# Context work in the first projection, weights split in the last turn of self-attention, later loads spread

## The reference

```python
x = x + attn(_layernorm(x)) @ w_out.T                         # self-attention, 2048 keys
x = x + cross(_layernorm(x), ctx_1024, ctx_1024, mask, ...)   # 154 context rows per batch
x = x + ffn(_layernorm(x), ...)                               # shared and selected experts
```

## Time and profile before

| | |
|---|---|
| median of 3 runs (range) | 3333.91 us (3328.81 to 3335.09) |
| the profiled execution | 3329.57 us, span 3327.8 us |
| busy in the span | PE 90%, DVE 66%, POOL 52%, ACT 49% |
| stage A | 0 to 314 us |
| stage B | 314 to 2138.5 us |
| stage C | 2138.5 to 2389.6 us |
| stage D | 2389.6 to 2430.4 us |
| stage E | 2430.4 to 2777.4 us |
| feed-forward stages | 2777.4 to 3327.8 us |

### The profile page before, as it was taken

One profiled execution on the slowest core, in us unless ns is written; L12 is line 12 of the kernel. 1 busy time (PEld: TensorE's weight loads), 2 busy tenths in 40 slices (PEclk: granted clock), 3 DMA queues, 4 the chain that ended last, 5 costly groups with the idle time before them and its releaser, 6 DMA issues. The chain is left out here.

```text
span 3327.8 us, 41873 instructions
## 1 busy us (share of the span) xinstructions
PE 2984.6 (90%) x15214; PEld 1715.5 (52%) x15214; DVE 2191.5 (66%) x3923; ACT 1620.7 (49%) x2965; POOL 1718.3 (52%) x693
## 2 busy tenths in 40 slices
PE   7997999999999999999999999499558995989478
PEld 6885444444444444444444444178434553777433
DVE  4333888788888888888888886156227894666323
ACT  2221366666666666666666666322116672222111
POOL 0001287888787888878787878500021001333265
PEclk9998699999999999999999999799769997999689
DMA  4445544655547446464464443468664343333621
GB/s 178 177 164 174 131 86 105 139 107 125 121 89 155 86 105 141 105 142 104 99 143 105 86 96 72 129 190 242 167 157 132 117 120 115 127 132 115 214 80 35
DMA packets 171869, 424.75 MB, mean 128 GB/s; under 512 B 19361, under 2 KB 40770, under 8 KB 151684
## 3 DMA queue, kind: packets, MB, share of 16 engines
q1 hardware_dynamic: 147550, 277.49, 28.6%
q0 software_dynamic: 24128, 144.75, 20.7%
HBM read 170.20 MB, written 124.58 MB: 89 GB/s over the span
## 5 line engine op out<-in xcount | busy, mean ns | idle before, releaser
L654 DVE TENSOR_REDUCE part_max<-ps_s 128x1 f32<-128x512 f32 x2048 | 1270.6, 680 | 308.7 <-PE ps_s L555 308.7
L751 ACT ACTIVATE probs<-ps_st 128x512 f32<-128x512 f32 x2048 | 1086.2, 601 | 547.0 <-PE ps_st L574 527.0
L513 POOL TENSOR_TENSOR added<-added,probs 128x2048 f32<-128x2048 f32 x256 | 1182.5, 4619 | 91.3 <-ACT probs L751 64.9
L555 PE MATMUL ps_s<-k_stack,q_stack 96*128 96x512 f32 x2048 | 841.5, 427 | 28.0 <-POOL max_parts L503 20.6
L574 PE MATMUL ps_st<-q_stack,k_stack 98*128 98x512 f32 x2048 | 858.2, 425 | 6.3 <-ACT probs L751 5.0
L574 PEld LDWEIGHTS ps_st<-q_stack,k_stack 98*128 98x128 f32 x2048 | 386.6, 190 | 505.3 <-ACT probs L751 362.8
L585 PE MATMUL ps_pv<-probs,v_sb 128*32 128x512 f32 x4096 | 546.3, 605 | 0.0
L555 PEld LDWEIGHTS ps_s<-k_stack,q_stack 96*128 96x128 f32 x2048 | 395.2, 193 | 214.8 <-DVE part_max L654 144.2
L521 POOL DMA_DIRECT2D probs<-probs x128 | 112.9, 882 | 231.6 <-PE ps_pv L585 219.3
L513 POOL TENSOR_TENSOR added<-probs 128x2048 f32<-128x2048 f32 x32 | 146.0, 4563 | 48.7 <-ACT probs L751 48.7
L679 DVE RECIPROCAL ps_d<-ps_d 128x128 f32<-128x128 f32 x128 | 120.9, 949 | 64.3 <-PE ps_d L600 64.3
(11 more groups left out here) (268 smaller groups left out, 3573.1 us busy)
## 6 DMA issues: line engine op xcount, KB each, us to landing
probs<-probs POOLq DMA_DIRECT2D x128, 1024.0 KB, 6.9
xq_stack<-q_parts SPq DMA_DIRECT2D x64, 384.0 KB, 4.5
q_stack<-q_hi SPq DMA_DIRECT2D x64, 256.0 KB, 6.0
k_stack<-k_hi SPq DMA_DIRECT2D x64, 256.0 KB, 8.1
q_parts<-q_h_out SPq DMA_DIRECT2D x64, 256.0 KB, 4.9
x_in<-in_x_rows SPq DMA_DIRECT2D x8, 1024.0 KB
q_hi<-qk_h_out SPq DMA_DIRECT2D x8, 1024.0 KB, 4.3
q_lo<-qk_l_out SPq DMA_DIRECT2D x8, 1024.0 KB, 6.4
```

The lines of the kernel that those rows point to most:

```text
L513: pool.tensor_tensor(added[:, w % 2], left, probs[:, k % RING], ALU.add).then_inc(added_up, 1)
L555: pe.matmul(ps_s[:, place % BANKS], q_stack[0:ROWS, w % 4, j, t * P:(t + 1) * P], k_stack[0:ROWS, w // BPB, j, n * BLK:(n + 1) * BLK], sta ...
L654: dve.tensor_reduce(part_max[:, s:s + 1], ps_s[:, (w * SLOTS + s) % BANKS], AX.X, ALU.max)\
L751: act.activation(probs[:, k % RING, j], ps_st[:, n % BANKS], ACT.Exp, scale=SCALE).then_inc(item_used, 1)
```

## The change

Stage D is gone. Its work goes into stage A: SP issues its ten loads behind the first block of x and the identity and ahead of the weights, and its stores behind the load of block 1; PE makes the keys before `transposes(0, 0)` and the values behind them; ACT adds the bias before `transposed(0, 0)`; POOL makes the high and low parts of the keys; DVE makes the masks between `norm(0, 0)` and `transposed(0, 0)`, and adds the values' bias between its weight splits. PSUM has two banks for it where stage D had eight. Stage B copies both weights of stage C to DRAM scratch at its start, loads them in the last turn at w = 3 into the free half of `k_stack`, with block 0 of the attention's output into that of `v_sb`; ACT makes their high parts in unit w = 6 at k = 4 and 11, DVE their low parts in w = 7. Stage C starts with the split of block 0. In stage E `load_q(2)` goes ahead of `rows_into_place(0)`, `load_q(3)` to u = 0, the batch-1 keys to u = 2 and 4, and the three weights to u = 6, 8 and 10.

```diff
# Ahead
-    def load(self, sp):
-        for source, raw, _, _ in self.weights:
-            sp.dma_start(raw, source).then_inc(self.loaded, 16)
+    def load(self, sp, n):
+        source, raw, _, _ = self.weights[n]
+        sp.dma_start(raw, source).then_inc(self.loaded, 16)
...
# project_qkv, SP
                 sp.dma_start(ident[:], eye).then_inc(ident_loaded, 16)
+                sp.dma_start(ctx_sb[:], weight_rows(ctx_t)).then_inc(ctx_loaded["k"], 16)
+                sp.dma_start(wk_sb, weight_rows(wk_t)).then_inc(ctx_loaded["k"], 16)
+                sp.dma_start(bk_sb[:], bk_cols).then_inc(ctx_loaded["k"], 16)
+                sp.dma_start(xwv_sb, weight_rows(xv_t)).then_inc(ctx_loaded["v"], 16)
+                sp.dma_start(bv_sb[:], bv.partition_broadcast(KH)).then_inc(ctx_loaded["v"], 16)
+                sp.dma_start(pad_col[:], pad_cols).then_inc(ctx_loaded["mask"], 16)
+                for b in range(B):
+                    sp.dma_start(pad_row[:, b], pad[b].partition_broadcast(P)).then_inc(ctx_loaded["mask"], 16)
+                sp.dma_start(cq, causal_q).then_inc(ctx_loaded["mask"], 16)
+                sp.dma_start(ck, causal_k).then_inc(ctx_loaded["mask"], 16)
...
                 sp.dma_start(x_in[:, 1], x_blocks[1]).then_inc(x_loaded[1], 16)
+
+                sp.wait_ge(k_low, B)
...
+                sp.wait_ge(v_ready, 2 * B)
+                sp.dma_start(xv_rows, xv[:]).then_inc(ctx_stored, 16)
+                sp.wait_ge(masks_done, 3 * B + 1)
...
# project_qkv, POOL
                 rsqrt(0)
+                pool.wait_ge(k_biased, DC)
+                for b in range(B):
+                    pool.tensor_copy(kt_h[:, b], kt[:, b]).then_inc(k_high, 1)
+                for b in range(B):
+                    pool.wait_ge(k_high, b + 1)
+                    pool.tensor_tensor(kt_l[:, b], kt[:, b], kt_h[:, b].bitcast(F32), ALU.subtract).then_inc(k_low, 1)
                 rsqrt(1)
...
# project_qkv, DVE (masks() is stage D's code)
+                def context_values(n):
+                    dve.wait_ge(ctx_v_done, n + 1)
+                    dve.wait_ge(ctx_loaded["v"], 32)
+                    dve.tensor_tensor(xv[:, n // 2, n % 2], ps_x[0:KH, n % 2], bv_sb[:], ALU.add).then_inc(v_ready, 1)
+
                 norm(0, 0)
+                masks()
                 transposed(0, 0)
+                for n in range(2):
+                    context_values(n)
                 for n, (raw, high, low) in enumerate(WEIGHTS):
                     dve.wait_ge(w_high, n + 1)
                     dve.tensor_tensor(low, raw, high.bitcast(F32), ALU.subtract).then_inc(w_low, 1)
+                    if n < 2:
+                        context_values(n + 2)
...
# project_qkv, PE
+                def context_keys(c):
+                    if c >= 2:
+                        pe.wait_ge(k_biased, c - 1)
...
+                def context_values(n):
+                    if n < 2:
+                        pe.wait_ge(k_biased, DC - 1 + n)
+                    else:
+                        pe.wait_ge(v_ready, n - 1)
...
+                pe.wait_ge(ctx_loaded["k"], 48)
+                for c in range(DC):
+                    context_keys(c)
                 pe.wait_ge(ident_loaded, 16)
                 transposes(0, 0)
+                pe.wait_ge(ctx_loaded["v"], 32)
+                for n in range(2 * B):
+                    context_values(n)
                 blocks(pe, body)
...
# self_attention, SP
+                        if last and w == BPB - 1:
+                            sp.wait_ge(next_w_copied, 32)
+                            for n in range(2):
+                                sp.dma_start(next_raw[:, n], weight_rows(next_w[n])).then_inc(next_w_loaded, 16)
+                            sp.wait_ge(pv_done, at(i, w, KT, KT))
+                            sp.dma_start(next_a, attn_t.rearrange("b (c p) (n k) -> b n p c k", p=P, k=BLK)[0, 0])\
+                              .then_inc(next_a_loaded, 16)
                         store(i, w)
...
                 load_v(1, 1)
+                for n, weights in enumerate((wo_t, wq_t)):
+                    sp.dma_start(next_w[n], weights).then_inc(next_w_copied, 16)
...
# self_attention, DVE and ACT
+                        if last and w == UPB - 1:
+                            for n in range(2):
+                                dve.wait_ge(next_high, n + 1)
+                                dve.tensor_tensor(next_l[:, n], next_raw[:, n], next_h[:, n].bitcast(F32), ALU.subtract)\
+                                   .then_inc(next_low, 1)
...
+                            if last and w == UPB - 2 and k in (4, 11):
+                                n = (4, 11).index(k)
+                                act.wait_ge(next_w_loaded, 32)
+                                act.activation(next_h[:, n], next_raw[:, n], ACT.Copy).then_inc(next_high, 1)
...
# attention_to_queries (SP: load_x(0, 0), identity, bias, load(1, 1)); DVE, ACT, PE
-                split_weights(0)
                 split(0, 0)
-                split_weights(1)
...
+                project(0, 0)
                 pe.wait_ge(small_loaded, 32)
-                pe.wait_ge(w_low, 2)
-                project(0, 0)
                 transposes(0, 0, range(TPB))
...
# cross_attention, SP
+        AHEAD_AT = (6, 8, 10)
...
+                load_q(2)
                 rows_into_place(0)
                 sp.dma_start(v_sb[:], xv_rows).then_inc(v_loaded, 16)
-                load_q(2)
-                load_q(3)
                 for u in range(UNITS + 3):
                     if exists(u + 1):
                         rows_into_place(u + 1)
                     if u == 0:
+                        load_q(3)
+                    elif u == 2:
                         load_scores_k(1)
+                    elif u == 4:
                         load_transposed_k(1)
-                        ahead.load(sp)
+                    elif u in AHEAD_AT:
+                        ahead.load(sp, AHEAD_AT.index(u))
```

More of the change, by code:

```diff
@@ L108, in project_qkv @@
         GROUPS = QK + TPB
+        ctx_sb = sb("ctx_sb", [P, DC, B * SC])
+        wk_sb, xwv_sb = (qk_l_out[:, n:n + DC].bitcast(F32) for n in (0, DC))
+        bk_sb = sb("bk_sb", [P, DC])
+        bv_sb = sb("bv_sb", [KH, D])
+        kt = v_out[:].rearrange("p t d -> p (t d)")[:, 0:B * DC * SC].rearrange("p (b c k) -> p b c k", b=B, c=DC)
+        kt_h = sb("kt_h", [P, B, DC, SC], F32R)
+        kt_l = sb("kt_l", [P, B, DC, SC], F32R)
+        xv = sb("xv", [KH, B, 2, D])
+        pad_col = sb("pad_col", [KH, B, 2], U8)
+        pad_row = sb("pad_row", [P, B, SC], U8)
+        bias_col = sb("bias_col", [KH, B, 2])
+        bias_row = sb("bias_row", [P, B, SC])
+        scaled_col = sb("scaled_col", [KH, B, 2])
+        cq = qk_h_out[:, 0:2].bitcast(F32).rearrange("p n k -> p (n k)")[:, 0:TPB * SC].rearrange("p (t k) -> p t k", t=TPB)
+        ck = qk_h_out[0:KH, 2:4].bitcast(F32)
+        mq = sb("mq", [P, B, TPB, SC], BF16)
+        mk = sb("mk", [KH, B, 2, BLK], BF16)
+        ps_x = ctx.enter_context(nc.psum_tensor("ps_ctx", [P, 2, BLK], F32))
+        ctx_loaded = {n: sem(f"ctx_{n}_loaded") for n in ("k", "v", "mask")}
+        ctx_k_done, ctx_v_done, k_biased, k_high, k_low, v_ready, bias_done, masks_done, ctx_stored = (
+            sem(n) for n in ("ctx_k_done", "ctx_v_done", "k_biased", "k_high", "k_low", "v_ready", "bias_done", "masks_done",
+                             "ctx_stored"))
         ident_loaded, w_high, w_low = sem("ident_loaded"), sem("w_high"), sem("w_low")
@@ L260, in group @@
                             act.wait_ge(stored["q_hi" if g == 0 else "k_hi"], count(i, u, 16, 0))
+                        if g == 0 and first(i, u):
+                            act.wait_ge(masks_done, 3 * B + 1)
                         out = qk_h_out[:, g]
                     else:
-                        if g == QK and not first(i, u):
+                        if g == QK and first(i, u):
+                            act.wait_ge(k_low, B)
+                        elif g == QK:
                             act.wait_ge(stored["v"], count(i, u, 16, 0))
@@ L272, in body @@
                         group(i, u, g)
+                act.wait_ge(ctx_loaded["k"], 48)
+                for c in range(DC):
+                    act.wait_ge(ctx_k_done, c + 1)
+                    act.activation(kt[:, :, c], ps_x[:, c % 2, 0:B * SC].rearrange("p (b k) -> p b k", b=B), ACT.Identity,
+                                   bias=bk_sb[:, c:c + 1]).then_inc(k_biased, 1)
                 transposed(0, 0)
@@ L814, in attention_to_queries @@
         small_loaded, consts = sem("small_loaded"), sem("consts")
-        w_loaded = [sem(f"c_w_loaded{n}") for n in range(2)]
-        w_high, w_low = sem("c_w_high"), sem("c_w_low")
         a_loaded, x_loaded = ([sem(f"c_{n}_loaded{s}") for s in range(2)] for n in ("a", "x"))
@@ L920, in split @@
                         dve.wait_ge(proj_done, count(i, u, TPB, 0))
```

(5 more changed lines are left out.)

186 lines of the change are left out of this document (59 added, 127 removed).

## The result

The changed kernel takes 3311.29 us (median of 8 runs, 3296.14 to 3315.79), the kernel before on the same chip 3331.69 us (3328.59 to 3340.1): a ratio of 0.9934, with a 95% interval from 0.992 to 0.9947. It is faster, but by 20 us where 47 were forecast, and it lies above the range. The profiled execution took 3310.81 us, 18.8 less than that of before.

The account below looks back on a forecast made before the run. PE was taken as busy for nine tenths of the span, losing time at seams between stages. Terms -40.9 + 15.8 - 14.0 + 3.3 - 11.5 = -47.3 gave 3282.3 (profiled) or 3286.6 (median); forecast 3284 us, range 3271 to 3299.

Parts of the forecast that it names:

- Stage D goes, -40.9: Between stages C and E: with stage D removed, stage E's first instruction comes 40.9 us earlier; the barrier stays.
- stage A takes it in, +15.8: Stage A's start: keys, masks and values come first, so group 1 begins at 42.2 instead of 26.44, +15.8 us.
- Stage C's start, -14.0: Stage C's start: PE begins at 2142.8 instead of 2156.77, after one ACT copy and one DVE subtraction, -14.0 us.
- Stage B, +3.3: Stage B's end: ACT's copies cost 0.5 us, DVE's subtractions holding up POOL's adds 2.8 us.
- Stage E, first and second idle time, half clock and `load_q(3)`: -16.3 together: Stage E: idle times vanish (-8.2, -8.1), half clock after the second shrinks (-2.3), waiting for `load_q(3)` costs +2.3 us.
- Stage E, POOL's split beside DVE, +4.8: Stage E, u = 10 to 13: DVE instructions wait for POOL's weight split while DVE has little free time, +4.8 us.
- late loads bring little: Rival, stage E: rows wait behind spread loads or `load_q(3)` is later; gain 3 instead of 11.5 us, 3293; chance 0.15.
- the slower one: Rival, stage E: each of five spread loads idles PE, then a unit at half clock; 61 us, 3345; chance 0.01.
- POOL and DVE shut each other out longer: Rival, stages B and E: each of POOL's waits adds up, 4.6 us in B, 10 in E; 3291; chance 0.15.
- The two rivals about stage A: Stage A costs all 25.2 us of PE, 3293, chance 0.08; or hides more and E gives 18, 3273, chance 0.1.

## Why the prediction was wrong

By its own steps, in the order of the sum:

- **Stage D goes, -40.9, and stage A takes it in, +15.8.** Right: 15.6 in the trace, 25.1 for both together by experiment against 25.1 on record. Keys at 11.32, masks at 19.31 and group 0 at 38.95 are within a microsecond and a half of what was worked out from stage D's rows.
- **Stage C's start, -14.0.** Right: 2157.46 is 0.7 later than before, in a kernel that had come there 14.6 later. What the step had no term for is where the weights lie: +2.3 over the stage.
- **Stage B, +3.3.** Right for the end of the stage, to which its reasons apply. POOL's five adds beside DVE's two subtractions took 27.54 us instead of the 23.49 that such a run takes, and from the start of these adds to stage C it is 2153.16 - 2065.21 = 87.95 us, where before it was 2138.53 - 2052.96 = 85.57: 2.4 more. In all profiled executions with the new stage B that stretch takes 86.7 to 88.0, in the three with the old one 84.5 to 85.6. The whole stage is even 1.0 us shorter in this pair, because its earlier part took 3.4 less; but that part varies by as much with the same code (1736.0 to 1741.4 us in the three old ones), so this is chance and not a gain.
- **Stage E, first and second idle time, half clock and `load_q(3)`: -16.3 together.** Right: without the split the stage is 323.6 - 307.1 = 16.5 us shorter (in this are the 1.2 us that the old split cost, which the prediction took off the next term). PE waits 2.58 us for `load_q(3)` where 2.3 was written.
- **Stage E, POOL's split beside DVE, +4.8.** This is the step that failed. It cost 35.4. (Already the 4.8 is not the middle of its own bounds: 3 to 10 less 3.2 has it at 3.3.) The delay itself, two long waits of DVE and 5.2 us of idle PE (0.95 and 4.27), was close to what the step had. But the step priced a stall of DVE at its own length. In PE's pause the clock went to 1.2 GHz, and it stayed there through the small matmuls of the unmasked units until the causal ones: 65 us, in which, by the 264 matmuls in 60 us above (36.4 us of work), 39% is lost, some 26. The prediction knew the clock's fall, from 4.6 us at 0.50 after the second idle time, and took that as what a fall costs in this stage. Those 4.6 us lie in the masked first units, where the clock comes back soon, as in the experiment with the split in the causal units. The row was real, and was carried to a part of the stage where it does not hold.

With 35.4 for 4.8, the pair's own -1.0 for 3.3 and the 2.3, the sum is -47.3 + 30.6 - 4.3 + 2.3 = -18.7, and the profiled executions differ by 18.8.

Of the rivals, the first (late loads bring little) and the slower one (each spread load stops PE) are refuted by the second stretch of the table above and by the kernel without the split. *POOL and DVE shut each other out longer* named the right place, with 10 us as its dearest case. The slower rival had the right mechanism, a pause and then half clock, with the wrong trigger, and ended its half clock after one unit. The two rivals about stage A are refuted by its 15.6 us.

The Trainium skill, page "SBUF — State Buffer", section "Who interferes with whom", has the exclusive lock between a DVE instruction with two inputs in SBUF and a GpSimd one that reads SBUF. The traces agree: DVE's multiplication, begun at 2542.87 beside POOL's subtraction of 4.58 us, ended 0.55 us after it, at 2546.03. The Trainium skill, page "TensorE: Matmul & The Clock Gate", section "HAM oscillation — how this bites in real kernels", tells of a kernel in which each wait for data takes the clock down, and the price is paid anew for each stretch of work. The trace agrees on the fall (in the pause of 4.27 us), but here one pause of 1.25 us was enough for 119 us at half clock without another pause. On that the measurement decides.

## What to carry to other kernels

Before you let another engine stall the one that paces TensorE, ask not only how long TensorE will idle but what it does afterwards: if matmuls like those of the unmasked units here follow (small tiles, none in bf16), one short pause may cost the clock until others come. Put work that locks DVE out where no matmuls are left, or beside dense ones, and read the price of a lost clock from the same kind of unit in which it would be lost. If a kernel's runs fall into two groups some 50 us apart with two mean clocks, such a stretch is worth looking for.

## What was not expected of the hardware

- A pause of 1.25 us was followed by 119 us at 1.2 GHz in the profiled execution, and the times of nine in ten runs say the same, but 1.23 us in the kernel before took nothing; the busy share of PE was 1.0 all that time. Sixteen matmuls of 128x128 or 98x77 by 512 in bf16 ended the same state within 4 us, sixteen of 77x32 didn't.
- Half clock lasted some 10 us where masked units followed (2594.7 to 2605 with the split in the causal units), and 65 to 119 us where unmasked ones did, 188 in the profiled run with the old stage E.
- The same matmul, 128x128 by 512, has a median of 389 ns with its weights in one place in SBUF and 396 in another, in two kernels that differ in nothing else.
